# A decoder layer on one core: the attention's 39 pipeline steps written out on every engine instead of a loop with registers

## The reference

```python
x = _layernorm(x + attn(x, Wq, Wk, Wv))                    # 16 query heads, one shared key/value head of 16
x = _layernorm(x + xattn(x, ctx, ctx, mask, W1, b1, W2, b2))  # 120 context rows per sequence
x = _layernorm(x + ffn(x, Wg, W1, b1, Wo, bo))             # 8 experts, each token goes to its best 2
```

## Time and profile before

| | us |
|---|---|
| median of 3 runs (lowest, highest) | 1499.45 (1497.93, 1501.52) |
| the profiled execution | 1495.7 |
| its span, first to last instruction | 1493.9 |
| PE busy in it | 1282.1 |
| DVE busy | 1142.6 |
| ACT busy | 756.8 |
| POOL busy | 656.1 |

### The profile page before, as it was taken

The page is one execution under the profiler, slowest core; times in us unless marked ns, Lnnn a source line. Parts: engine busy times, 40 slices in busy tenths (PEclk is TensorE's granted clock), DMA queues, the critical chain, the costliest instruction groups (busy, mean ns, idle before and its releaser), DMA issues. The chain is left out here.

```text
span 1493.9 us, 32343 instructions
## 1 busy us (share of the span) xinstructions
PE 1282.1 (86%) x7668; PEld 903.5 (60%) x7669; DVE 1142.6 (76%) x3110; ACT 756.8 (51%) x1743; POOL 656.1 (44%) x1018
## 2 busy tenths in 40 slices
PE   6888999989899898989988505999999999968886
PEld 4443555555555555555543304888888888858786
DVE  1455788888788787878874467888888888859998
ACT  1125677777677677777777241323223232314444
POOL 1011244444454444444544472334343343447886
PEclk9998999999999999999998557999999999989999
DMA  4435456647556566566535721433434334369995
GB/s 100 105 60 100 80 107 131 122 103 131 114 113 126 113 119 116 119 124 112 118 87 181 273 94 58 133 135 130 137 128 136 131 129 138 129 239 318 338 331 200
DMA packets 171805, 211.34 MB, mean 141 GB/s; under 512 B 20048, under 2 KB 143056, under 8 KB 167632
## 3 DMA queue, kind: packets, MB, share of 16 engines
q1 hardware_dynamic: 147808, 143.92, 41.7%
q0 software_dynamic: 17680, 55.28, 9.9%
q10 hardware_dynamic: 6240, 11.34, 2.2%
HBM read 124.81 MB, written 84.89 MB: 140 GB/s over the span
## 5 line engine op out<-in xcount | busy, mean ns | idle before, releaser
L859 DVE TENSOR_REDUCE negmax<-psS 128x2 f32<-128x512 f32 x512 | 349.6, 687 | 109.0 <-PE psS L631 102.0
L761 ACT ACTIVATE probs<-psT 128x512 f32<-128x512 f32 x512 | 302.7, 597 | 190.3 <-PE psT L641 189.4
L631 PE MATMUL psS<-kstack,qstack 96*128 96x256 bf16 x1024 | 197.4, 275 | 50.7 <-DVE negmax L859 21.6
L1337 ACT ACTIVATE sig<-hb 128x512 f32<-128x512 f32 x136 | 86.0, 633 | 287.2 <-DVE hb L1420 281.6
L641 PE MATMUL psT<-qstack,kstack 99*128 99x512 bf16 x512 | 197.2, 386 | 5.1 <-ACT probs L761 5.1
L1217 POOL DMA_INDIRECT g_rows<-g,slot x136 | 135.5, 996 | 70.2 <-issue 66.9
L631 PEld LDWEIGHTS psS<-kstack,qstack 96*128 96x128 bf16 x1024 | 92.0, 104 | 109.9 <-DVE negmax L859 74.0
L397 POOL DMA_INDIRECT lists<-x,slots x128 | 127.0, 992 | 34.2 <-issue 30.3
L529 PE MATMUL psO<-probs,vaug 128*32 128x512 f32 x1024 | 140.0, 619 | 0.9 <-ACT probs L761 0.8
L1431 DVE SCALAR_TENSOR_TENSOR g<-g,xe,sig 128x512 f32<-128x512 f32 x136 | 102.3, 752 | 27.4 <-DVE g L1427 14.4
L1420 DVE TENSOR_TENSOR hb<-psHb,f_b 128x512 f32<-128x512 f32 x136 | 94.1, 692 | 36.6 <-issue 31.8
(11 more groups left out here) (201 smaller groups left out, 2962.8 us busy)
## 6 DMA issues: line engine op xcount, KB each, us to landing
rows<-g_rows SPq DMA_DIRECT2D x32, 1024.0 KB, 8.1
qstack<-q_parts SPq DMA_DIRECT2D x192, 128.0 KB
xe<-lists SPq DMA_DIRECT2D x136, 133.0 KB, 2.1
q_parts<-qpart SPq DMA_DIRECT2D x32, 384.0 KB, 2.8
sums<-x SPq DMA_DIRECT2D x32, 264.0 KB, 2.3
x2in<-sums SPq DMA_DIRECT2D x32, 264.0 KB, 5.0
xt<-in_x_t SPq DMA_DIRECT2D x32, 256.0 KB, 6.0
xres<-in_x SPq DMA_DIRECT2D x32, 256.0 KB, 3.2
```

What stands on the lines that cost most here:

```text
L631: last = mm(psS[:, u % 2, hh * S:(hh + 1) * S], qstack[0:KROWS, b1.s4, 2 * hp + hh, c * P:(c + 1) * P], kstack[0:KROWS, b1.s4, :], start=T ...
L761: nc.scalar.activation(probs[:, u % PT, :], psT[:, u % 2, :], ACT.Exp, scale=SELF_SCALE).then_inc(sm["exp_done"], 1)
L859: v.tensor_reduce(negmax[:, b1.s2, 2 * hp:2 * hp + 2, c], psS[:, u % 2, :].rearrange("p (h k) -> p h k", h=2), AX.X, ALU.max, negate=True) ...
```

## The change

`pipeline` of the attention phase is now one Python loop over 39 constant step numbers. No engine has a loop there any more: the branch is gone, all waits and addresses of `t` = 8 to 31 hold constants, and the register instructions are gone. In these 24 steps `bank_read` still waits for the last user of a bank alone. The steps written out before are as they were. The experts phase keeps its loops.

```diff
     def pipeline(eng, step):
 
-
-        for r in range(8):
-            step(Step(0, r))
-        with eng.Fori(2, B // 4) as j:
-            for r in range(4):
-                step(Step(j, r))
-        for r in range(7):
-            step(Step(B // 4, r))
+        for n in range(B + 7):
+            step(Step(0, n))
 
...
             order = list(bank)
             i = order.index(use)
-            for k in range(len(order)) if t.fixed else ((i - 1) % len(order),):
+            for k in range(len(order)) if not 8 <= t.n < B else ((i - 1) % len(order),):
                 name, lag, per, nth = bank[order[k]]
```

## The result

The changed kernel takes 1474.32 us (median of 4 runs, 1472.99 to 1477.75), the kernel before 1498.69 us (4 runs, 1492.17 to 1501.52). The ratio is 0.9844, with an interval from 0.9804 to 0.9884.

The account below looks back on a forecast made before the run. A ring of hand-overs between PE, DVE and ACT was taken as the bound. Branches 13.7 plus registers 4.8 give 18.5 us, so 1495.7 becomes 1477.2, and with the median's 3.75 us offset 1481.0; range 1476 to 1488.

Parts of the forecast that it names:

- The ring: Attention steps: hand-overs between PE, DVE and ACT, with neither PE nor DVE full, set the step, 22.07 us in the loop.
- Term 1, the branches: Five backward branches of the attention loop: DVE stops to fetch code; removing them gains 13.7 us, 2.7 us each.
- term 2: Register instructions at three hand-overs in 24 steps: removing them gains about 0.2 us a step, 4.8 us in all.
- Straight code costs nothing: Attention code written out: fetching it is covered by code fetched ahead and priced at nothing.
- The rival at 1569: Fetching straight code stops an engine, 1.77 us for each of 50 packets: slower, 1569 us; chance 0.03.
- more than both: Hand-overs not priced, such as ACT before L569, also shorten: 0.3 us a step or more, 1478 us or below; chance 0.10.
- Branches only: Removing registers in the attention steps gains zero, only the branches' 13.7 us count: 1485.7 us; chance 0.28.
- The explanation of why written-out step 7 was no shorter: Written-out step 7 waits for all users of the bank between L900 and L594, losing 0.23 us despite having no registers.
- Stops move: DVE waits for code at a few block ends instead of at branches: 1495 to 1499 us; chance 0.07.

## Why the prediction was right, and what failed

**What bounds the kernel.** Right. The ring sets the step before and after, no instruction became shorter, and the length between two L884 held the effect: 19.5 of 21.0 us of the pair of profiles.

**Term 1, the branches: right mechanism, wrong size.** In the pair of profiles it is 543.38 - 523.90 - 5.7 (term 2) = 13.8 us, as forecast. That this pair agrees is luck, since the profile was the cheapest of three. The step that failed is "So the five branches cost 455.12 - 441.4 = 13.7 us, 2.7 us each", together with the step that carried it from one execution to a median, "with the same offset the median becomes 1481.0". One profile stood for the kernel. Its three profiles give 13.8, 18.2 and 24.8 us, 18.9 on average. With term 2 that is 24.6 us, beside medians that differ by 24.4, 29.1 and 29.3 us. The second thing missed is why it spreads: the steps with a branch have a nearly fixed price of 2.3 to 3.1 us each, and then PE's clock may fall behind them. The earlier trace rows had it in view (PEclk 0.98 in one stretch, 91.60 us against 90.66), and the prediction used it only as something that would vanish.

In numbers, the measured median lies 6.7 us below the forecast, and 4.9 of these come from the offset: the profiled execution of before lay 3.75 us below its median, and the prediction gave the changed kernel the same offset, but that kernel's profiled execution lies 1.16 us above its median. The pair of profiled executions differs by 1495.70 - 1475.48 = 20.2 us, 1.7 more than the forecast 18.5, and the medians by 20.2 + 3.0 (1498.69 - 1495.70) + 1.2 = 24.4 us.

The timed executions bear out that the kernel before loses at the clock in varying amounts. Of its 23 on the last chip, the six with a mean granted clock of 0.943 or less took 1502.8 to 1515.3 us and the nine with 0.951 or more 1493.2 to 1499.0 us. The changed kernel's six on that chip have 0.952 to 0.954 each. This mean is over the whole span, so it doesn't say how much of it falls behind a branch.

That the stop is DVE's own fetching is supported by the 19 packets, by the branch to the next code that costs nothing, and by the twelve-step body. The Trainium skill's rule in Runtime: NRT & Kernel Launch, "Instruction fetch mechanics" (a taken branch to a page that isn't held forces a fetch), was on the right side: it names no such fetch for code that goes straight on. The loops that are walked once agree, with 523.94 us beside 523.90.

**Straight code costs nothing.** Right: 9 and 10 packets arrive from 285 to 460 us, and all steps from 8 to 31 are 21.8 us. The rival at 1569 needed more than 0.37 us a packet; no such cost is to be seen.

**Term 2, the registers.** Mechanism right, size somewhat low: 22.07 - 21.82 = 0.25 us (0.245 before rounding) for each of 23 steps and 22.05 - 21.98 = 0.07 for step 7, 5.7 us in all, forecast 0.2 and 4.8. The seam gave 0.16 (taken 0.15), L945 to L859 0.09 (0.09), L900 to L594 lost 0.07 (0.05). That makes 0.18 us. A hand-over that I hadn't priced would fill the missing 0.07, from ACT's second L683 to PE's L569. That the gains add up in this way wasn't tested. In order of time, first before, then after (where they are L677 and L563):

```profile
263.67 1.10 ACT L683 ACTIVATE x<-y,shift,rstd 128x256 f32<-128x256 f32 x2
...
264.89 0.42 PEld L569 LDWEIGHTS psB<-ident,x 128*128 128x128 f32 x4 [1.33 <-DVE qrest L884]
```

```profile
260.80 1.10 ACT L677 ACTIVATE x<-y,shift,rstd 128x256 f32<-128x256 f32 x2
...
261.95 0.42 PEld L563 LDWEIGHTS psB<-ident,x 128*128 128x128 f32 x4 [1.26 <-ACT x L677]
```

It is 264.89 - 264.77 = 0.12 us before and 261.95 - 261.90 = 0.05 us after. That was the content of the rival "more than both", at a quarter of its size. "Branches only" fell, as the steps are not 22.07. The explanation of why written-out step 7 was no shorter held in the main: with all six waits in every step 0.17 of the 0.25 us are gone again.

**Stops move.** Fell: no step from 8 to 31 is longer than its neighbours, in three profiles, and PEclk is 1.00. The sign that the prediction named, no idle time ended by "issue" in front of the old L867, is there too, but at L853 the label comes and goes between profiles with no effect on the steps.

**What stays open.** The size of the branches' cost rests on three profiles of the kernel before. Their profiled executions took 1493.7 to 1495.7 us, below the medians of 1495.4 to 1501.4 of all its executions, and on the whole span the three profiles of each kernel differ by 20.9 us on average, not by 24.6. So 3.5 to 8.4 us of the medians' difference are not seen in the profiles' spans. Why the clock falls at some branches and not at others after stops of like length isn't settled. A loop whose DVE body is short enough to stay in place wasn't tried, nor was ACT alone written out.

## What to carry to other kernels

Before costing a loop's branches, look at which engine stops behind them with "issue", who waits for it, and whether the step gets longer, since idle times with that label also stand where they cost nothing; write out that engine alone first, since here DVE alone gave nearly all of the gain. Where a stop leaves PE idle, compare several profiles before sizing it: here the stop repeated, but what the clock made of it didn't. A hand-over in a ring can be lengthened by the instructions ahead of the waiting one, waits and registers alike, and here the single wait kept two thirds of what the constants brought. Before moving work, check that the engine has no slack at that place.

## What the runs showed of the hardware

Pauses of PE of about 2 us, made by a late DVE, can bring its clock from 1.00 to 0.50 about 1.5 us after it has resumed, for about 13 us, and turn a loss of 2.3 us into one of 8 us. With the stop put in by hand the clock fell too (0.50 from 666 to 672 us), and one of five stops lengthened the next step as well, by 2.3 us. Engines differ in when a backward branch stops them: with bodies of four steps DVE alone, with bodies of twelve also PE (3.4 us) and ACT (2.7 us). A hardware loop that is walked once costs nothing that 24 steps can show, 523.94 us against 523.90.
